# Expert step of a mixture-of-experts layer: transposes of rows and of h side by side, h one step later

## The reference, cut to what matters

```
g = jax.lax.ragged_dot(xs, w_gate, group_sizes)
u = jax.lax.ragged_dot(xs, w_up, group_sizes)
d = jax.lax.ragged_dot(jax.nn.silu(g) * u, w_down, group_sizes)
...
expert_out = jnp.sum(out * weights[..., None], axis=1)
shared = jax.nn.silu(x @ sw_gate) * (x @ sw_up) @ sw_down
return (expert_out + shared).reshape(B, S, H)
```

## Time and profile before

| | |
|---|---|
| median of 3 runs | 892.03 us |
| profiled execution | 893.14 us |
| its span | 891.2 us |
| TensorE busy, whole span | 741.9 us (83%), 6832 matmul records |
| VectorE, ScalarE, GpSimd busy | 473.9, 294.9, 209.2 us |
| the expert stage on TensorE | about 640 to 847 us |
| mean granted clock of TensorE | 0.952 of 2.4 GHz |

### The profile page before, as it was taken

One profiled execution on the slowest core, in us unless ns is written; L12 is line 12 of the kernel. 1 busy time (PEld: TensorE's weight loads), 2 busy tenths in 40 slices (PEclk: granted clock), 3 DMA queues, 4 the chain that ended last, 5 costly groups with the idle time before them and its releaser, 6 DMA issues. The chain is left out here.

```text
span 891.2 us, 18175 instructions
## 1 busy us (share of the span) xinstructions
PE 741.9 (83%) x6832; PEld 457.1 (51%) x6887; DVE 473.9 (53%) x1240; ACT 294.9 (33%) x702; POOL 209.2 (23%) x253
## 2 busy tenths in 40 slices
PE   3589987877799999999999998699699999999900
PEld 3457765555554455655566666467344433434400
DVE  5755565566448886455453454259533333333447
ACT  0013233444420102333333333233265544555400
POOL 3111222010000000000000000054456556665500
PEclk9999999999969999999999999879899999999955
DMA  9493002000000000000000000087122222222273
GB/s 295 122 293 110 2 3 95 1 3 1 2 1 1 0 1 1 1 1 2 2 1 2 1 3 1 1 224 214 32 75 84 78 84 80 82 84 78 73 244 103
DMA packets 48123, 55.28 MB, mean 62 GB/s; under 512 B 7366, under 2 KB 43174, under 8 KB 47334
## 3 DMA queue, kind: packets, MB, share of 16 engines
q1 hardware_dynamic: 38246, 34.11, 13.2%
q0 software_dynamic: 6656, 16.85, 5.6%
q10 hardware_dynamic: 3136, 3.15, 1.1%
HBM read 41.45 MB, written 12.65 MB: 61 GB/s over the span
## 5 line engine op out<-in xcount | busy, mean ns | idle before, releaser
L730 DVE TENSOR_REDUCE nmf<-bank 128x4 f32<-128x512 f32 x192 | 123.7, 686 | 123.6 <-PE bank L336 123.5
L590 ACT ACTIVATE pt<-bank 128x512 f32<-128x512 f32 x192 | 104.2, 595 | 252.8 <-PE bank L356 252.8
L336 PE MATMUL bank<-kk,qT 32*128 32x256 f32 x768 | 109.2, 401 | 15.9 <-ACT pt L590 8.3
L928 POOL TENSOR_TENSOR rstd<-vare,half 128x1 f32<-128x1 f32 x32 | 17.5, 546 | 376.9 <-DVE vare L791 376.9
L336 PEld LDWEIGHTS bank<-kk,qT 32*128 32x128 f32 x768 | 67.2, 184 | 51.2 <-issue 35.3
L1531 PE MATMUL bank<-wgu,g_xgT 128*64 x256 | 90.5, 476 | 2.1 <-ACT g_xgT L1568 1.2
L1531 PE MATMUL bank<-g_wgu,g_xgT 128*64 128x352 f32 x256 | 90.5, 476 | 0.0
L356 PE MATMUL bank<-nm,sel 32*128 32x128 f32 x768 | 84.5, 338 | 0.0
L1496 POOL DMA_INDIRECT out_rows<-g_og,g_out_row x64 | 63.9, 998 | 64.9 <-DVE g_og L1600 54.5
L348 PE MATMUL bank<-qT,kk 32*128 32x512 f32 x256 | 74.6, 659 | 2.0 <-ACT pt L590 1.5
L1551 PE MATMUL bank<-wd,g_hT 128*64 x256 | 68.9, 392 | 0.2
(11 more groups left out here) (242 smaller groups left out, 1346.5 us busy)
## 6 DMA issues: line engine op xcount, KB each, us to landing
wgu<-in_L_ffn_w_gate SPq DMA_DIRECT2D x4, 1408.0 KB
wgu<-in_L_ffn_w_up SPq DMA_DIRECT2D x4, 1408.0 KB
wd<-in_L_ffn_w_down SPq DMA_DIRECT2D x32, 176.0 KB
g_y<-out_rows SPq DMA_DIRECT2D x4, 768.0 KB, 16.7
g_y<-out_rows ACTq DMA_DIRECT2D x4, 768.0 KB, 17.4
sparse_table<-f_m_re SPq DMA_DIRECT2D x2, 1024.0 KB
f_m_re<-sparse_table SPq DMA_DIRECT2D x2, 1024.0 KB, 5.9
f_idx_row<-in_L_ffn_mask_idx SPq DMA_DIRECT2D x1, 1024.0 KB
```

The costliest lines, as they stand in the source:

```text
L336: return pe.matmul(bank, q, k, start=first, stop=r == 1, skip_group_check=True)
L590: act.activation(T.pt[2 * (t % 2) + u][:, :], STB[u][:, :], ACT.Exp, scale=own[v].scale).then_inc(exp_done, 1)
L730: dve.tensor_reduce(T.nmf[v % 2][:, 2 * (c % 2) + u, at:at + 4], SB[u][:, :].rearrange("p (h k) -> p h k", h=4), AX.X, ALU.max, negate=Tru ...
```

## The change

TensorE's `step(c)` becomes: transposes of x for c + 2, transposes of h for c - 1 (not c), gate/up for c + 1, down for c - 1. So h of a step is transposed one step later than before, directly behind the transposes of x, and it is transposed and multiplied by down in the same step. ScalarE's `step(c)` becomes: the register load, copy of x for c + 2, copy of h for c - 1, copy of weights for c + 2 (not c + 3), silu for c + 1. VectorE and GpSimd stay as they are. Waits and updates are the same ones, at their new places.

```diff
--- before.py
+++ after.py
@@ -1519,6 +1519,14 @@
                     for j in range(KT):
                         last = pe.transpose(trx[n % 2][:, j * 128:(j + 1) * 128], G.xg[n % 4][:, j * 128:(j + 1) * 128], T.ident[:])
                     last.then_inc(xt_done, 1)
+                n = c - 1
+                if has(n):
+                    pe.wait_ge(h_ready, n + 1)
+                    if n >= 2:
+                        pe.wait_ge(ht_ready, n - 1)
+                    for j in range(2):
+                        last = pe.transpose(trh[n % 2][0:MH, j * 128:(j + 1) * 128], G.h[n % 2][:, j * MH:(j + 1) * MH], T.ident[:])
+                    last.then_inc(tr_done, 1)
                 n = c + 1
                 if has(n):
                     pe.wait_ge(xt_copied, n + 1)
@@ -1531,14 +1539,6 @@
                             last = pe.matmul(gu[n % 2][rows, 0:2 * MI], G.xgT[n % 2][:, j * 128:(j + 1) * 128][:, rows], w,
                                              start=(j == 0), stop=(j == KT - 1), skip_group_check=True)
                     last.then_inc(gu_done, 1)
-                n = c
-                if has(n):
-                    pe.wait_ge(h_ready, n + 1)
-                    if n >= 2:
-                        pe.wait_ge(ht_ready, n - 1)
-                    for j in range(2):
-                        last = pe.transpose(trh[n % 2][0:MH, j * 128:(j + 1) * 128], G.h[n % 2][:, j * MH:(j + 1) * MH], T.ident[:])
-                    last.then_inc(tr_done, 1)
                 n = c - 1
                 if has(n):
                     pe.wait_ge(ht_ready, n + 1)
@@ -1564,22 +1564,22 @@
             def step(c):
                 n = c + 2
                 if has(n):
+                    unit = act.value_load(G.unit[0:1, SHARE * n + 1:SHARE * n + 2], min_val=0, max_val=UNITS - 1)
                     act.wait_ge(xt_done, n + 1)
                     act.activation(G.xgT[n % 2][:], trx[n % 2][:, 0:D], ACT.Copy).then_inc(xt_copied, 1)
+                n = c - 1
+                if has(n):
+                    act.wait_ge(tr_done, n + 1)
+                    act.activation(G.hT[n % 2][0:MH, :], trh[n % 2][0:MH, 0:256], ACT.Copy).then_inc(ht_ready, 1)
+                n = c + 2
+                if has(n):
+                    if n >= 2:
+                        act.wait_ge(gu_done, n - 1)
+                    act.activation(G.wgu[n % 2][:], T.wgu[:, bass.ds(unit, 1), :, :].rearrange("p a k n -> p (a k) n"), ACT.Copy).then_inc(wgu_ready, 1)
                 n = c + 1
                 if has(n):
                     act.wait_ge(gu_done, n + 1)
                     act.activation(G.sil[n % 2][:], gu[n % 2][:, 0:MI], ACT.Silu).then_inc(sil_ready, 1)
-                n = c
-                if has(n):
-                    act.wait_ge(tr_done, n + 1)
-                    act.activation(G.hT[n % 2][0:MH, :], trh[n % 2][0:MH, 0:256], ACT.Copy).then_inc(ht_ready, 1)
-                n = c + 3
-                if has(n):
-                    if n >= 2:
-                        act.wait_ge(gu_done, n - 1)
-                    unit = act.value_load(G.unit[0:1, SHARE * n + 1:SHARE * n + 2], min_val=0, max_val=UNITS - 1)
-                    act.activation(G.wgu[n % 2][:], T.wgu[:, bass.ds(unit, 1), :, :].rearrange("p a k n -> p (a k) n"), ACT.Copy).then_inc(wgu_ready, 1)
 
             act.wait_ge(T.low_loaded, T.low_count)
             act.wait_ge(T.high_loaded, T.high_count)
```

## The result

The changed kernel takes 900.26 us (median of six runs, 897.27 to 903.31), the kernel before 892.17 us beside it (six runs): a ratio of 1.0106, 95% interval 1.0077 to 1.0135. It is slower. Run again on a second chip, where the kernel before takes 901.69 us, the changed one takes 903.33 us: 1.0032 (1.0002 to 1.0062). The forecast was 895 against 892.03 us, a ratio of 1.0033, with 874 to 906 as its range. The sign is right on both chips, the size on the second; on the first it was 5 us short. (The ratios and their intervals are those on record; the plain quotients of the medians are 1.0091 and 1.0018.)

The account below looks back on a forecast made before the run. TensorE's own rhythm was taken to bound the stage, with late updates tied to GpSimd's DMA loop. From 893.1 us profiled, loop +1.5 and end +1.2 gave 895.8; less 1.1 for unprofiled runs, 895 us, range 874 to 906.

Parts of the forecast that it names:

- The rhythm: TensorE's quiet step: fewer tile-shape boundaries save 0.27 to 0.28 us, 3.07 to 2.79 us; 17.6 us over 63 steps.
- Rival 5: Transposes of h beside x still cost 0.34 us, so only 0.15 us a step goes; better half shares 0.17 chance.
- The loop: GpSimd's four indirect DMAs plus a pause make two steps take at least 6.45 us: +1.5 us over 56 steps.
- the end: Last two steps: nothing covers the copy of h, twice 0.93 instead of 0.34 us before down; +1.2 us.
- (a): Expert steps: late updates cost what they cost now, so 893.1 - 17.6 + 1.2 = 876.7 us.
- The slack: Copy of h between its transposes and down: spare time shrinks from 2.5 to 0.46 us, enough only in quiet steps.
- Way (c): Expert steps: ScalarE's 29.4 us idle in 18 waits, less 0.46 each, counted as added delay; 892.2 to 899.7 us.
- 1 (the rhythm wins, 875.6): Expert steps: the shorter step's gain comes through in full, 875.6 us; chance 0.24.
- holdups: Expert steps: other engines hear TensorE's updates late, some 3 us for down's eviction, while GpSimd issues indirect DMAs in a row.
- 2 (a stop ends the holdup sooner): Expert steps: idle TensorE may cut late updates short, leaving half of 17.6 us; 884.4 us, chance 0.17 including a half-rival.
- 3 (903): Every second step stops ahead of down for g_hT: +10 us, with the end 903, or +33; chance 0.18.
- 4: TensorE's granted clock may drop to 1.2 GHz if it rests 1 to 2 us per step pair; 915 or more, chance 0.05.

Follow-up runs that it names:

- e3_before_sp: Kernel before with the scatter taken off GpSimd: SyncE writes the rows to consecutive places by plain DMA (wrong places); 890.15 us, ratio 0.988.
- e4_after_sp: Changed kernel with the scatter taken off GpSimd: SyncE writes the rows to consecutive places by plain DMA (wrong places); 872.90 us, ratio 0.9704.
- e1_down_later: Changed kernel with down, its eviction and its scatter one step later, so the copy of h has a whole step again; 903.89 us, ratio 1.0042.
- p2_pad: Changed kernel with two unused transposes added ahead of those of x in each step; 909.32 us, ratio 1.0102.
- q_gather_later: Changed kernel with GpSimd's gather for step n waiting for gate/up of step n-4 instead of its transposes of x; 901.78 us, ratio 1.0003.
- g1_gather_sp: Changed kernel with the gather taken off GpSimd: SyncE loads consecutive rows by plain DMA (wrong rows); 875.67 us, ratio 0.9738.
- r_before: Kernel before, unchanged, run again with a trace on the second chip; 899.97 us, ratio 0.9989.
- e2_h_early: Changed kernel with h of step c, not c - 1, transposed behind the transposes of x; 908.33 us, ratio 1.0084.

## Why the prediction was right, and where it was not

**The rhythm** was right to 0.01 us. Forecast: 0.27 to 0.28 us a step less, 2.79 in a quiet step. The profile of the changed kernel shows 2.78, and the pair e3_before_sp and e4_after_sp 0.278 a step with nothing else in the way. The intervals are as forecast too: 0.27 from the first transpose of x to those of h, 0.31 to gate/up, 0.29 from its last matmul to down. Rival 5 is out, and the intervals show where the gain is made: at the two boundaries between tile shapes that the new order doesn't have. That the change of shape itself is what costs there is argued from the earlier trace rows; no run tests it apart from the order.

**The loop** was right in what it forecast: two steps at 6.44 us where 6.45 stood, a stage 1.75 us longer of which 0.55 in steps 7 to 63 (forecast 1.5) and the rest around it, mostly the end: 1.00 (forecast 1.2). The argument against (a), that with steps of 2.79 the next down ends while GpSimd still issues, is what the changed kernel shows at 705.32. That the loop and not the slack sets the price is shown by e1_down_later: the slack back, the price the same. But it was called a period of its own, and it isn't one: p2_pad stretches it to 6.68, q_gather_later turns it into 9.63 for three. The rows say why the two kernels agree: 4.84 us from the first issue of a row of four to the end of the last (701.45 to 706.29), 0.89 to the eviction, 0.71 to the next issue, 6.44 together, with the same row of four in the earlier trace rows. In p2_pad the row has a pause of 0.51 for 0.30 us in its middle, and the loop is 6.65 (700.72 to 707.37). So the loop is GpSimd's row plus the hold behind it; it sets the pair of steps for as long as four issues stay together. Over all kernels with both indirect issues and no work added the mean step is 3.20 to 3.31 us, and GpSimd is busy for some 60% of it (107.97 of 179.49 us; before 108.58 of 179.41). What holds the updates inside the chip no run shows.

**The slack** was mis-sized. In a quiet step the copy of x starts 0.47 us after the first transpose (703.09 to 702.62), not 0.61, and the copy of h 0.28 behind that (0.75 in e4_after_sp's rows too), not 0.89 after the transpose. The way from the end of that copy to TensorE was put at about 0.1 us and took 0.15 (707.88 to 708.03, where down's first weight load starts). With down due 1.81 after the first transpose the slack is 0.54, not 0.46, and in the held step down came 0.83 late for a copy of x that was 1.36 late, which is 0.53. The 0.08 us more changed nothing, as a whole step more in e1_down_later didn't.

**Way (c)** came out near the forecast by other numbers. It took the old waits of ScalarE, 29.4 us in 18, as the lateness to come. There are 28 stops of 0.87 us instead, 24.4 us, and 56 x 2.78 + 24.4 = 180.1 against 179.5 measured. A lateness read from the old profile isn't a cost that can be carried over, since it adapts to the step.

**The rivals.** 1 (the rhythm wins, 875.6) is what would happen without holdups: e4_after_sp has 872.9, g1_gather_sp 875.7. Its condition failed, not its sum. 2 (a stop ends the holdup sooner) fell half: the lateness did shrink, down's update from some 3 us to 1.67, because TensorE stands still and the next down comes later; but the pair of steps takes as long. 3 (903) came closest: every second step stops ahead of down, as it says, and it put the stop at which that decides at 0.84 us, 28 times. The stops are 0.87 us. They stand at break-even, not beyond it, since the two loops are of one length. 4: in the changed kernel the granted clock is 1.00 through steps 7 to 63 on both chips, with TensorE standing for 10 to 12% of the time. The mechanism isn't empty, though: the clock did fall once among these steps in r_before (behind a stop of 1.95 us) and in e2_h_early (during one of 3.31 us), for 3.4 and 6.8 us. The changed kernel's stops are shorter, 0.6 to 0.8 us of idle time, a few of up to 1.4.

**The step that failed**, as far as the first chip's size goes, is the base of the sum. It started from the profiled execution and held all outside the stage fixed; 4.4 us of the first chip's 6.3 arose there, ahead of the first gather, with the clock at its lower level for longer. The chances took 0.2% as what a measurement can tell from no change. That was too little: the ratio of the first chip and that of the second differ by 0.74 points.

**What was to show it.** "More than 20 us ahead of down" was 17.1 in the groups and 19.0 in the table of waits on the first chip, close but under, and 21.4 on the second; the 5 us that would have refuted it are far away. Evictions 6.4 us apart in pairs: 702.73, then 707.18 and 709.22 on the next two, so a pair 6.49 long. The mean step of 3.205 is under the 3.35 that would have meant rival 3.

## What to carry to other kernels

Before a rhythm is shortened, look for a second loop that runs beside it at nearly the same length: here four issues of another engine and a pause, 6.45 us for two steps, against 6.14 of TensorE's own. A gain in the rhythm then turns into a stop, wherever the slack is least, and giving slack back only moves the stop (17.1 us ahead of down, 17.8 ahead of gate/up, 23.4 ahead of the transposes of h). Test what the loop is made of by taking one of its members away before the order is changed: with the scatter off GpSimd the same change of order is worth 0.278 us a step, with it on GpSimd nothing.

No kernel here that leaves the rows as they should be beats the one before: q_gather_later is level with it. The faster ones, at 0.97 to 0.99, show what a scatter or a gather with fewer or cheaper indirect issues would be worth; how to get the rows to their places that way was not tried.

## What was not expected of the hardware

- TensorE's updates came late while GpSimd issued indirect DMAs without a pause, by 1.64 us in the mean for those due during the fourth in the changed kernel. These came about 0.9 us after the last issue of the row had ended; those of gate/up, due during the third, came 0.4 us late while the row still ran. TensorE itself went on meanwhile, until it came to a wait for the late copy.
- In this stage it took two indirect issues a step: 0.97 to 0.99 us each for 128 rows. A plain DMA from GpSimd is 0.59 us, and with it and a pause of 0.92 us in each step nothing was late. A pause of 0.51 us in p2_pad was not enough.
- 128*64 matmuls of gate/up lead into 128*64 matmuls of down at the usual 0.29 us. Into whole-array transposes they took 0.40 before.
- The same program took 892 us on one chip and 901 to 902 on three others, 1.1%, which is as much as the change is worth on the first and more than it is on the second.
